# A transformer tower on one Trainium2 core: GpSimd adds two bias rows to whole tiles instead of TensorE passes with a selector row

## The chip, the cores and the metric

The kernel runs on one core of a Trainium2 chip. The metric is the time of one execution in microseconds, taken on the device. The engines are named TensorE (PE in the profile, PEld its weight loads), VectorE (DVE), ScalarE (ACT), GpSimd (POOL) and SyncE (SP, which here only starts DMAs).

## What is computed

A sequence of 129 rows (one class row, 128 rows made from the input by a state-space kernel) of 64 steps and 1024 columns goes through one layer: a layer norm, a narrow mixer (down to 128 columns, two rounds of a bidirectional state-space block, up to 1024), a residual, a second layer norm, and a feed-forward part of a base product plus routed low-rank experts. Cut to what touches the change:

```
def attn(x, ...):                    # x = layernorm(h)
    h = gelu(x @ w_down.T + b_down)
    ...                              # two state-space rounds, gate
    h = h @ w_up.T + b_up            # <- up bias
    return x + h

def ffn(x, ...):                     # x = layernorm(h)
    base_out = x @ base_W.T + base_b # <- base bias
    probs = softmax(x @ router_W.T + router_b)
    ...                              # top 8 of 15, low-rank experts
    return base_out + lora

h = tok(x, ...)
h = concat([cls_tok, h])
h = h + attn(layernorm(h), ...)
h = h + ffn(layernorm(h), ...)
```

## The kernel before

A tile is 128 partitions (two rows of the sequence, 64 steps each) by 1024 columns; there are 65 tiles, the last with the class row. The kernel is one software pipeline over iterations i = 0 to 69. In iteration i, tile i is made and normed (part A), tiles i-1 and i-2 are in the state-space rounds (H and G), tile i-4 gets its up product, residual and second norm (D), and tile i-5 its feed-forward part and its store (E). Iterations 8 to 61 stand in a loop of two, the others are written out. Every engine has its own hand-written order of steps, printed below at the end of each `body`, and waits on semaphores named after the steps (`wait(pool, i, tt=1)`: until tile i has its first `tt`).

The names that matter:

- `T` (two buffers): the new tile. GpSimd's `carry_h` (L908) makes `T * SD1 + NM1` of it, which is tile plus its first norm; the semaphore is `tt`. SP stores T to HBM (L801) and fetches it three iterations later as `T2` (L792). `carry_h` is the last step of GpSimd's iteration; ahead of it stand two decay products, `decays_back` (RB, L925), and additions of the narrow convolution, `add_bc`. Behind it the next iteration begins with `swap` (XSW, L846), `kernel_q` (V2, L853), `gram_back` (NB), `shift_imag`, `shift_none` and `skip` (XD, L885).
- `up` (TensorE, L1579): for each half of the columns four passes into one bank, the first of which is `mm(bT, row_sel, up_bias[:, c])`. `residual` (VectorE, L1401) adds the bank to `T2` and writes `HB`.
- `HB` (two buffers): what comes out of the first half. `norm_2` (ScalarE, L1016) norms it into T2, semaphore `xh2`. `turn_d` transposes that, and ScalarE and VectorE split it into `XHI` (`split_hi`) and `XLO` (`split_lo`, L1428).
- `bases` (TensorE, L1558): for each half of the columns 24 passes into bank `bO[h]`, and ahead of them `mm(bO[h], row_sel, base_bias[:, c])`. It waits for `xlo=2` of its tile.
- `final` (VectorE, L1448): adds `bO[h]` to HB, in place; SP then stores HB (L826). In VectorE's order, the end of an iteration is `split_lo(0)`, `final(0)`, `final(1)`, `split_lo(1)`; the next begins with `kernel_p` (VB, L1226), the gram products, `kernel_sum`, the mixing matrix Mt (L1287), and soon `add_skip` and `times_z` (XD).
- `mix` (TensorE, L1723) needs Mt. `turn_x` (L1647) transposes the input and needs XSW.

`row_sel` has ones in rows 0 and 32 and zeros elsewhere. Rows 0 and 32 of the 128-row tiles `up_bias` and `base_bias` hold the high and the low part of the bias, so that one TensorE pass lays the whole bias row on all 128 partitions of a bank. The prologue builds these: two loads to 64 rows, two ScalarE copies (L454, L455), two GpSimd subtractions (L345).

Of the kernel before, what the change touches and what calls it, by code (L numbers as in the profile page):

```python
# [38 lines left out]
def build(nc, x, cls_tok, log_dt, tok_B, inv_A_real, A_imag, w_down, b_down, w_up, b_up, gate1, in_w,  # L55
# [14 lines left out]
    BCP = 48  # L70
    BIAS_ROWS, BIAS_LO = 64, 32
    TILES = pairs + 1
    CLS = pairs

    with ExitStack() as keep:
# [23 lines left out]
        m_gt = sb("m_gt", [P, CS])  # L99
        row_sel = sb("row_sel", [P, P], F32R)  # L100
        up_bias = sb("up_bias", [P, HID], F32R)
        base_bias = sb("base_bias", [P, HID], F32R)
        rbias = sb("rbias", [P, NR])
# [31 lines left out]
        with ExitStack() as tmp:  # L135
# [18 lines left out]
            ones = ts("ones", [P, P])  # L154
            bias_s = ts("bias_s", [BIAS_ROWS, 2, HID])
            earlier0 = ts("earlier0", [P, P])
# [36 lines left out]
            s_zero, s_masks, s_consts = tsem("s_zero"), tsem("s_masks"), tsem("s_consts")  # L193
            s_bias, s_sel = tsem("s_bias"), tsem("s_sel")
            s_dup, s_par, s_tdt, s_exps = tsem("s_dup"), tsem("s_par"), tsem("s_tdt"), tsem("s_exps")
# [39 lines left out]
            def _(sp):  # L235
# [14 lines left out]
                for c in range(2):  # L250
                    small(cw[:, c, :], cwr[c * P:(c + 1) * P, :])
                    small(cb[:, c:c + 1], conv_b[c * P:(c + 1) * P].unsqueeze(1))
                small(bias_s[:, 0, :], b_up.unsqueeze(0).broadcast_to([BIAS_ROWS, HID]))
                small(bias_s[:, 1, :], base_b.unsqueeze(0).broadcast_to([BIAS_ROWS, HID]))
                small(rbias[:, :], router_b.unsqueeze(0).broadcast_to([P, NR]))
# [32 lines left out]
            def _(pool):  # L288
# [22 lines left out]
                for k, s in enumerate((512, 256, 768)):  # L311
                    pool.iota(lst_i[:, 32 + k:33 + k], pattern=[[1, 1]], base=s,
                              channel_multiplier=0).then_inc(s_consts, 1)
                pool.memset(row_sel[:, :].bitcast(F32), 0.0).then_inc(s_sel, 1)
                pool.memset(up_bias[:, :].bitcast(F32), 0.0).then_inc(s_sel, 1)
                pool.memset(base_bias[:, :].bitcast(F32), 0.0).then_inc(s_sel, 1)
                pool.wait_ge(s_sel, 3)
                for k, row in enumerate((0, BIAS_LO)):
                    pool.memset(row_sel[row:row + 1, :].bitcast(F32), 1.0).then_inc(s_sel, 1)
                    pool.wait_ge(s_sel, 4 + k)  # L320
                pool.memset(half_neg[:, :], -0.5)
# [19 lines left out]
                pool.wait_ge(s_onehot, NE)  # L341
                pool.wait_ge(s_bias, 2)
                for k, dst in enumerate((up_bias, base_bias)):
                    lo = slice(BIAS_LO, BIAS_ROWS)
                    link(TT(dst[lo, :], bias_s[lo, k, :], dst[lo, :].bitcast(F32), ALU.subtract))  # L345
                pool.wait_ge(s_albe, 1)
# [36 lines left out]
            def _(act):  # L383
# [58 lines left out]
                for c in range(CHUNKS):  # L442
                    if c % 2 == 0:
                        waves(c)
                        falls(c)
                    else:
                        falls(c)
                        waves(c)
                    if c == 0:
                        act.wait_ge(s_small, 16 * NSMALL)  # L450
                        act.wait_ge(s_sel, 3)
                        act.activation(alog[:, :], alog[:, :], ACT.Exp).then_inc(s_exps, 1)
                        act.activation(gt0[:, :], gate[:, :], ACT.Exp, scale=-1.0).then_inc(s_exps, 1)
                        act.activation(up_bias[0:BIAS_ROWS, :], bias_s[:, 0, :], ACT.Copy).then_inc(s_bias, 1)  # L454
                        act.activation(base_bias[0:BIAS_ROWS, :], bias_s[:, 1, :], ACT.Copy).then_inc(s_bias, 1)  # L455
                        while k < SMALL_JOBS:
                            nxt = evacuate(k, nxt)
                            k += 1
                    for _ in range(PER_CHUNK):
                        nxt = evacuate(k, nxt)  # L460
                        k += 1
# [5 lines left out]
            def _(dve):  # L467
# [156 lines left out]
                for c in range(CHUNKS):  # L624
# [82 lines left out]
        per = dict(cls_in=(1, 16), xswap=1, xt=1, xtc=1, wr=1, wi=2, wsum=1, v1=1, v2=1, vsum=1,  # L707
                   km=2, hev=4, st1=4, rs1=1, sd1=1, nm1=1, xh1=1, tt=1, tr1=2, xte=2, down=1, gelu=1,
                   pin=3, xms=1, conv0=4, conv=NCONV, cbm=TAPS - 1, cbc=TAPS - 1, dtc=NDT, asp=2, edt=1, xs=3, sz=1, trx=1, gram=1, xse=1,
# [60 lines left out]
        with nc.Block() as block:  # L770

            @block.sync
            def _(sp):
                def body(i, p):
                    if active(i, -1, CLS + 1) and not (isinstance(i, int) and not 1 < i + 1 < CLS):
                        load_x(i + 1, 1 - p)
                    if isinstance(i, int) and i == CLS:

                        wait(sp, i - 2, xh1=1)
                        wait_carry(sp, i - 2, p)  # L780
                        sp.dma_start(T[:, p, :], cls_tok[0].broadcast_to([P, HID])).then_inc(S["cls_in"].sem, 16)
                    if active(i, 5, TILES):
                        store(i - 5, 1 - p)
                    if active(i, 3, TILES):
                        src = at(carried, i - 3)

                        wait_carry(sp, i - 3, 1 - p)
                        wait(sp, i - 4, tr2=2)
                        apart(sp)
                        wait(sp, i - 4, gt=1)  # L790
                        apart(sp)
                        inc(sp.dma_start(T2[:, :], src[:, 0:HID]), "fetched")  # L792
                        inc(sp.dma_start(XM[:, :], src[:, HID:HID + P]), "fetched")
                    if active(i, 0, TILES):
                        dst = at(carried, i)
                        wait(sp, i, gelu=1)
                        apart(sp)
                        sp.dma_start(dst[:, HID:HID + P], U[:, p, 0, :]).then_inc(carry[p], 16)
                        wait(sp, i, tt=1)
                        apart(sp)  # L800
                        sp.dma_start(dst[:, 0:HID], T[:, p, :]).then_inc(carry[p], 16)  # L801
# [31 lines left out]
            def _(pool):  # L833
                def body(i, p):
# [65 lines left out]
                    def deviation_1():  # L900

                        if A1:
                            wait(pool, i, rs1=1)
                            wait(pool, i - 1, tt=1)
                            apart(pool)
                            inc(pool.tensor_scalar(SD1[:, :], RS1[:, :], 1.0, 1.0, ALU.mult, ALU.add), "sd1")

                    def carry_h():  # L908

                        if A1:  # L910
                            wait(pool, i, sd1=1, nm1=1, xh1=1)
                            apart(pool)
                            inc(pool.tensor_scalar(T[:, p, :], T[:, p, :], SD1[:, 0:1], NM1[:, 0:1], ALU.mult, ALU.add), "tt")

                    def root_2():
                        if D:
                            wait(pool, td, st2=4)
                            wait(pool, td - 1, xh2=1)
                            inc(pool.tensor_tensor(RS2[:, :], VE2[:, :], half_neg[:, 0:1], ALU.pow), "rs2")  # L919

                    def decays_back(part):
# [31 lines left out]
                    decays_back(1)  # L953
                    carry_h()


# [204 lines left out]
            def _(dve):  # L1161
                TT, TS, STT = dve.tensor_tensor, dve.tensor_scalar, dve.scalar_tensor_tensor

                def body(i, p):
# [209 lines left out]
                    def shift_1():  # L1374

                        if A1:
                            wait(dve, i, rs1=1)
                            wait(dve, i - 1, xh1=1, tt=1)
                            inc(STT(NM1[:, :], MV1[:, 0:1], -1.0, RS1[:, 0:1], ALU.mult, ALU.mult), "nm1")
# [68 lines left out]
                    def final(h):  # L1448
                        if E:
                            wait(dve, te, o=h + 1)  # L1450
                            c = slice(HALF * h, HALF * (h + 1))
# [79 lines left out]
            def _(pe):  # L1531
                mm, tr = pe.matmul, pe.transpose

                def body(i, p):
# [6 lines left out]
                    def ffn(c0, c1, bank, ks, last=None):  # L1541

                        for k in ks:
                            for n, (xs_, ws) in enumerate(((XHI, w_hi), (XHI, w_lo), (XLO, w_hi))):
                                ins = mm(bank[:, 0:c1 - c0], xs_[:, 1 - p, k, :], ws[:, k, c0:c1],  # L1545
                                         start=(c0 == HID and k == 0 and n == 0), stop=(last == k and n == 2))
                        return ins
# [10 lines left out]
                    def bases(h, a, b):  # L1558
                        if E:
                            if a == 0:  # L1560
                                wait(pe, te, xlo=2)
                                wait(pe, te - 1, fin=h + 1)
                                mm(bO[h][:, :], row_sel[:, :], base_bias[:, HALF * h:HALF * (h + 1)], start=True, stop=False)
                            ffn(HALF * h, HALF * (h + 1), bO[h], range(a, b))
# [14 lines left out]
                    def up(h):  # L1579
                        if D:  # L1580
# [5 lines left out]
                            c = slice(HALF * h, HALF * (h + 1))  # L1586
                            mm(bT[:, :], row_sel[:, :], up_bias[:, c], start=True, stop=False)
                            mm(bT[:, :], GTS[:, 0, :], wu_hi[:, c], start=False, stop=False)
                            mm(bT[:, :], GTS[:, 1, :], wu_hi[:, c], start=False, stop=False)
# [239 lines left out]
```

## Time and profile before

| what | before |
|---|---|
| median of 3 runs | 2318.59 us |
| lowest, highest | 2317.51, 2318.93 us |
| span of the profiled execution | 2315.8 us |
| TensorE busy | 2160.1 us, 93% |
| VectorE busy | 1843.7 us, 80% |
| ScalarE busy | 1527.5 us, 66% |
| GpSimd busy | 1095.6 us, 47% |

The profiled execution is a run of its own; only its span is known, the time from its first to its last instruction. Times in the timelines count from the start of the span. In a timeline row the columns are: start, duration, engine, line, operation, tiles written <- read, shape, count, and in brackets the idle time of the engine before it with what ended it. A TensorE pass is shown with its whole latency; the pitch, the distance between two starts, is what it costs in a row of passes. The granted clock is given as a share of 2.4 GHz; its two levels here are 1.0 and 0.5 (1.2 GHz).

### The profile page before, as it was taken

Reading aid. Unit: us, or ns where it says so; the run is one execution under the profiler, and the core shown is the slowest. Engines: PE = TensorE matmul, PEld = TensorE weight load, DVE = VectorE, ACT = ScalarE, POOL = GpSimd, SP = SyncE. Lnnn points to the kernel's source line nnn. Section 1 sums busy time; section 2 is a strip of 40 time slices with the busy share of each in tenths; the row PEclk is TensorE's granted clock in tenths of the full one; section 3 lists DMA queues with packets and bytes.
Section 4 is the critical chain, followed back from the end, with each engine's and each line's share of the span. In section 5 each row is a group of like instructions: output and inputs, shape, how many; then the busy total and the mean of one; then the engine's idle time right before and its main releaser. Section 6 shows DMA issues by size and latency. Waiting matters only on the chain.

```text
span 2315.8 us, 51899 instructions
## 1 busy us (share of the span) xinstructions
PE 2160.1 (93%) x14117; PEld 1805.7 (78%) x14117; DVE 1843.7 (80%) x4980; ACT 1527.5 (66%) x2921; POOL 1095.6 (47%) x1350
## 2 busy tenths in 40 slices
PE   2366999999999999999999999999999999999997
PEld 2245888888888888888888888888888888888776
DVE  8666788888888888888888888888888888887763
ACT  4465676667766677666777667676676766767552
POOL 5543554445544455444554445544455444554321
PEclk8577999999999999999999999999999999999999
DMA  5201111222112221122221222212222112221111
GB/s 150 65 26 36 56 51 47 64 64 64 50 46 64 64 64 58 37 64 64 64 61 35 64 64 64 63 34 61 64 64 64 35 60 64 64 64 38 62 40 34
DMA packets 90061, 132.61 MB, mean 57 GB/s; under 512 B 20379, under 2 KB 63559, under 8 KB 90006
## 3 DMA queue, kind: packets, MB, share of 16 engines
q1 hardware_dynamic: 87496, 126.12, 18.4%
q10 hardware_dynamic: 2510, 5.83, 0.8%
q8 instruction: 25, 0.41, 0.1%
q14 instruction: 30, 0.25, 0.0%
HBM read 55.17 MB, written 76.74 MB: 57 GB/s over the span
## 4 chain that ended last, share of the span: by engine, by line
issue 44%; PE 27%; POOL 9%; DVE 7%; ACT 6%; POOLq 1%; DVEq 0%; ACTq 0%
PE bank L1644 5%; PE bank L1545 5%; POOL CB L934 4%; PE bank L1600 3%; PE bank L1575 2%; DVE NF L1274 2%; ACT L1039 2%; POOL XD L885 2%; PE bank L1718 2%; PE bank L1702 2%; POOL RS L919 1%; PE bank L1577 1%; PE bank L1576 1%; POOL RS L898 1%; PE bank L1692 1%
## 5 line engine op out<-in xcount | busy, mean ns | idle before, releaser
L1545 PE MATMUL bank<-w_hi,XHI 128*128 128x512 f32 (+1 forms) x1560 | 623.0, 399 | 0.0
L1545 PE MATMUL bank<-w_lo,XHI 128*128 128x512 f32 (+1 forms) x1560 | 555.1, 356 | 0.0
L1545 PE MATMUL bank<-w_hi,XLO 128*128 128x512 f32 (+1 forms) x1560 | 554.6, 355 | 0.0
L1180 DVE SCALAR_TENSOR_TENSOR CX<-bank,cw,CX 128x252 f32<-128x252 f32 (+5 forms) x804 | 335.6, 459 | 62.2 <-ACT CX L977 62.0
L934 POOL TENSOR_TENSOR CB<-CB,CM 48x252 f32<-48x252 f32 (+5 forms) x402 | 293.1, 729 | 153.5 <-ACT CM L962 142.6
L1545 PEld LDWEIGHTS bank<-w_hi,XLO 128*128 128x128 f32 x1560 | 295.5, 189 | 46.9
L1545 PEld LDWEIGHTS bank<-w_lo,XHI 128*128 128x128 f32 x1560 | 297.0, 190 | 41.2
L1545 PEld LDWEIGHTS bank<-w_hi,XHI 128*128 128x128 f32 x1560 | 296.7, 190 | 41.2
L962 ACT ACTIVATE T<-bank 64x512 f32<-64x512 f32 x256 | 151.4, 591 | 261.9 <-PE bank L1634 257.2
L898 POOL TENSOR_TENSOR RS<-VE,half_neg 128x1 f32<-128x1 f32 x65 | 35.5, 546 | 370.7 <-DVE VE L1372 370.7
L925 POOL TENSOR_TENSOR RB<-m_gt,AS 128x512 fp32r<-128x512 f32 x134 | 165.0, 1231 | 56.9 <-DVE AS L1446 56.9
L962 ACT ACTIVATE CM<-CR,cwb 48x256 f32<-48x256 f32 x402 | 181.4, 497 | 3.7 <-POOL CB L934 1.5
L892 POOL TENSOR_TENSOR RS<-MS,half_neg 128x2 f32<-128x2 f32 x67 | 46.9, 700 | 244.2 <-DVE MS L1303 244.2
L1634 PE MATMUL bank<-VB,W 128*128 128x256 f32 x512 | 149.4, 416 | 7.8 <-DVE W L1245 5.8
L1428 DVE TENSOR_TENSOR XLO<-bank,XHI 128x512 fp32r<-128x512 f32 x130 | 89.9, 692 | 73.1 <-ACT XHI L962 73.1
L1434 DVE TENSOR_TENSOR RF<-m_lt,AS 128x512 fp32r<-128x512 f32 x134 | 142.8, 1104 | 0.0
L962 ACT ACTIVATE XHI<-bank 128x512 fp32r<-128x512 f32 x130 | 77.6, 597 | 95.3 <-PE bank L1600 95.3
L1644 PE MATMUL bank<-XHT,wdT 128*128 128x128 f32 x1040 | 135.4, 286 | 4.5 <-ACT XHT L962 4.5
L1644 PEld LDWEIGHTS bank<-XHT,wdT 128*128 128x128 f32 x1040 | 129.2, 202 | 6.1 <-ACT XHT L962 6.1
L877 POOL TENSOR_TENSOR NB<-GB,sp_dt 128x512 f32<-128x512 f32 x67 | 96.0, 1433 | 77.5 <-DVE GB L1257 77.5
L885 POOL TENSOR_TENSOR XD<-XS,DD 128x512 f32<-128x512 f32 x67 | 84.7, 1264 | 98.5 <-DVE DD L1265 53.2
L1292 DVE TENSOR_TENSOR XD<-bank,XD 128x512 f32<-128x512 f32 x67 | 46.4, 692 | 79.1 <-POOL XD L885 58.2
(295 smaller groups left out, 5375.1 us busy)
## 6 DMA issues: line engine op xcount, KB each, us to landing
carried<-T SPq DMA_DIRECT2D x65, 512.0 KB, 4.7
T<-carried SPq DMA_DIRECT2D x65, 512.0 KB, 3.8
out<-HB SPq DMA_DIRECT2D x129, 256.0 KB, 3.2
tables<-tab SPq DMA_DIRECT2D x8, 560.0 KB, 4.1
TB<-tables SPq DMA_DIRECT2D x64, 70.0 KB, 2.7
carried<-U SPq DMA_DIRECT2D x65, 64.0 KB, 3.5
XM<-carried SPq DMA_DIRECT2D x65, 64.0 KB, 4.7
XI<-in_x SPq DMA_DIRECT2D x128, 32.0 KB, 2.7
```

Of the source, the lines that this page charges most:

```text
L877: inc(pool.tensor_tensor(NB[:, :, :].rearrange("p (a h) t -> p a h t", a=2), GB[:, :, :].unsqueeze(2).broadcast_to([P, 2, NH, CS]), dtB, A ...
L885: inc(pool.tensor_tensor(XD[:, :, :], v3(XS[:, :], HD), DD[:, :].unsqueeze(2).broadcast_to([P, 2 * NH, HD]), ALU.mult), "xd")
L925: inc(pool.tensor_tensor(RB[:, part, :, :], m_gt[:, :].unsqueeze(1).broadcast_to([P, 2 * NH, CS]), decays(1, part), ALU.mult), "rb")
L934: inc(pool.tensor_tensor(CB[:, :, s:CS], CB[:, :, s:CS], CM[:, s % 3, :, 0:CS - s], ALU.add), "cbc")
L962: inc(act.activation(dst, src, ACT.Copy, scale=scale), name)
L1180: inc(STT(CX[:, c, :, s:CS], src[:, :, 0:CS - s], cw[:, c, k:k + 1], CX[:, c, :, s:CS], ALU.mult, ALU.add), "conv")
L1428: inc(TT(XLO[:, p, ks, :], v3(bT[:, :], P), XHI[:, p, ks, :].bitcast(F32), ALU.subtract), "xlo")
L1434: inc(TT(RF[:, part, :, :], m_lt[:, :].unsqueeze(1).broadcast_to([P, 2 * NH, CS]), decays(0, part), ALU.mult), "rf")
L1545: ins = mm(bank[:, 0:c1 - c0], xs_[:, 1 - p, k, :], ws[:, k, c0:c1], start=(c0 == HID and k == 0 and n == 0), stop=(last == k and n == 2))
L1600: ins = tr(bT[:, P * k:P * (k + 1)], T2[:, (4 * g + k) * P:(4 * g + k + 1) * P], ident[:, :])
L1634: ins = mm(bK[:, 256 * s:256 * (s + 1)], W[:, b, 2 * s:2 * s + 2, :].rearrange("p a c -> p (a c)"), VB[:, b, :, :].rearrange("p a c -> p ( ...
L1644: ins = mm(bK[:, 0:P], wdT[:, k, :], XHT[:, k, :], start=(k == 0), stop=(k == KC - 1))
```

## The change

The selector passes and all that builds them go. `up_bias` and `base_bias` become plain f32 tiles that hold the bias on all 128 partitions, loaded by DMA. GpSimd adds `up_bias` to T right behind the scaling in `carry_h` (so `tt` counts two), and `base_bias` to HB of tile i-5 in a new last step, `add_bias`, semaphore `hb`. All that waited for `tt=1` of a tile waits for `tt=2`: the carry store of SP, `deviation_1` of GpSimd and `shift_1` of VectorE for the tile after. `final` also waits for `hb`. In `bases` and `up` the first product pass now starts the accumulation.

```
-                small(bias_s[:, 0, :], b_up.unsqueeze(0).broadcast_to([BIAS_ROWS, HID]))
-                small(bias_s[:, 1, :], base_b.unsqueeze(0).broadcast_to([BIAS_ROWS, HID]))
+                small(up_bias[:, :], b_up.unsqueeze(0).broadcast_to([P, HID]))
+                small(base_bias[:, :], base_b.unsqueeze(0).broadcast_to([P, HID]))
...
-                        wait(sp, i, tt=1)
+                        wait(sp, i, tt=2)
...
                             inc(pool.tensor_scalar(T[:, p, :], T[:, p, :], SD1[:, 0:1], NM1[:, 0:1], ALU.mult, ALU.add), "tt")
+                            wait(pool, i, tt=1)
+                            inc(pool.tensor_tensor(T[:, p, :], T[:, p, :], up_bias[:, :], ALU.add), "tt")
...
+                    def add_bias():
+
+                        if active(i, 5, TILES):
+                            wait(pool, i - 5, xh2=1)
+                            inc(pool.tensor_tensor(HB[:, 1 - p, :], HB[:, 1 - p, :], base_bias[:, :], ALU.add), "hb")
...
                     decays_back(1)
                     carry_h()
+                    add_bias()
...
                         if E:
-                            wait(dve, te, o=h + 1)
+                            wait(dve, te, o=h + 1, hb=1)
                             c = slice(HALF * h, HALF * (h + 1))
                             inc(TT(HB[:, 1 - p, c], bO[h][:, :], HB[:, 1 - p, c], ALU.add), "fin")
...
-                                         start=(c0 == HID and k == 0 and n == 0), stop=(last == k and n == 2))
+                                         start=(k == 0 and n == 0), stop=(last == k and n == 2))
...
-                                mm(bO[h][:, :], row_sel[:, :], base_bias[:, HALF * h:HALF * (h + 1)], start=True, stop=False)
...
-                            mm(bT[:, :], row_sel[:, :], up_bias[:, c], start=True, stop=False)
-                            mm(bT[:, :], GTS[:, 0, :], wu_hi[:, c], start=False, stop=False)
+                            mm(bT[:, :], GTS[:, 0, :], wu_hi[:, c], start=True, stop=False)
```

## Rows read from the trace of the kernel before

**Rows 1.** The page's first part: busy time, share of the span, instructions.

```profile
PE 2160.1 (93%) x14117; PEld 1805.7 (78%) x14117; DVE 1843.7 (80%) x4980; ACT 1527.5 (66%) x2921; POOL 1095.6 (47%) x1350
```

**Rows 2.** Busy time by stretch: length, engines, granted clock, DMA share, GB/s.

```profile
1003.30:1067.50 64.20, 63.82 (x427) 53.70 (x427) 53.10 (x147) 44.81 (x87) 31.55 (x38) 1.00 0.19 57
```

**Rows 3.** Timeline of GpSimd at the seam of iterations 28 and 29.

```profile
1013.79 1.04 POOL L925 TENSOR_TENSOR RB<-m_gt,AS 128x512 fp32r<-128x512 f32 x1
1014.83 1.19 POOL L913 TENSOR_SCALAR T<-T,SD,NM 128x1024 f32<-128x1024 f32 x1
1015.97 0.29 POOL L846 COPY XSW<-XI 128x128 f32<-128x128 f32 x1
1016.22 1.06 POOL L853 TENSOR_TENSOR V<-TB 128x512 f32<-128x512 f32 x1
```

**Rows 4.** Timeline of VectorE, same seam.

```profile
1014.77 1.28 DVE L1452 TENSOR_TENSOR HB<-bank,HB 128x512 f32<-128x512 f32 x2
1016.29 0.69 DVE L1428 TENSOR_TENSOR XLO<-bank,XHI 128x512 fp32r<-128x512 f32 x1 [0.24 <-ACT XHI L962]
1016.90 0.93 DVE L1226 TENSOR_TENSOR VB<-TB 128x512 f32<-128x512 f32 x1
...
1018.15 0.68 DVE L1232 TENSOR_TENSOR VB<-VB,V 128x512 f32<-128x512 f32 x1
...
1021.55 0.69 DVE L1287 TENSOR_TENSOR Mt<-NF,EX 128x512 f32<-128x512 f32 x1
...
1025.11 0.69 DVE L1297 TENSOR_TENSOR XD<-XD,SZ 128x512 f32<-128x512 f32 x1
```

**Rows 5.** Timeline of TensorE, same seam, to `mix`.

```profile
1018.28 0.48 PE L1563 MATMUL bank<-base_bias,row_sel 128*128 128x512 f32 x1
1018.60 0.39 PE L1545 MATMUL bank<-w_hi,XHI 128*128 128x512 f32 x1
1018.83 0.40 PE L1545 MATMUL bank<-w_lo,XHI 128*128 128x512 f32 x1
...
1023.03 1.15 PE L1730 MATMUL bank<-XS,Mt 64*64 64x64 f32 x32
```

**Rows 6.** Timeline of ScalarE, same seam: evacuations of T, then squares.

```profile
1025.28 1.21 ACT L962 ACTIVATE T<-bank 64x512 f32<-64x512 f32 x2 [3.93 <-PE bank L1634]
1026.39 0.40 ACT L1060 ACTIVATE SQ<-XD 128x256 f32<-128x256 f32 x1
```

**Rows 7.** Timeline of GpSimd in the prologue: subtraction of two full operands.

```profile
30.80 2.36 POOL L345 TENSOR_TENSOR up_bias<-bias_s,up_bias 32x1024 fp32r<-32x1024 f32 x1
```

**Rows 8.** Busy time by stretch, columns as in rows 2: fill and tail.

```profile
181.60:188.40 6.80, 6.24 (x42) 5.21 (x43) 2.90 (x6) 2.09 (x6) 1.35 (x1) 0.50 0.01 2
...
215.70:219.10 3.40, 3.40 (x31) 2.87 (x27) 1.95 (x3) 0.14 (x1) 1.35 (x1) 0.51 0.00 0
...
2202.30:2205.70 3.40, 3.40 (x15) 3.01 (x13) 2.14 (x4) 2.47 (x3) 1.55 (x1) 0.50 0.92 241
```

**Rows 9.** Timeline of TensorE in the fill: `mix` behind an idle stretch.

```profile
182.16 1.98 PE L1730 MATMUL bank<-XS,Mt 64*64 64x64 f32 x32 [3.75 <-DVE Mt L1287]
...
215.29 1.62 PE L1730 MATMUL bank<-XS,Mt 64*64 64x64 f32 x32 [3.75 <-DVE Mt L1287]
```

**Rows 10.** Timeline of GpSimd: `carry_h` of iterations 5 and 64.

```profile
277.26 1.19 POOL L913 TENSOR_SCALAR T<-T,SD,NM 128x1024 f32<-128x1024 f32 x1
...
2168.77 1.21 POOL L913 TENSOR_SCALAR T<-T,SD,NM 128x1024 f32<-128x1024 f32 x1
```

**Rows 11.** Timeline of VectorE: `final` of iterations 5 and 64.

```profile
277.11 1.28 DVE L1452 TENSOR_TENSOR HB<-bank,HB 128x512 f32<-128x512 f32 x2
...
2168.62 1.28 DVE L1452 TENSOR_TENSOR HB<-bank,HB 128x512 f32<-128x512 f32 x2
```

**Rows 12.** Timeline of SyncE's queue at the seam of iterations 28 and 29.

```profile
1016.27 1.24 SPq L826 DMA_DIRECT2D out<-HB  x2
1018.07 0.36 SPq L792 DMA_DIRECT2D T<-carried  x1
```

More of the change, by code:

```diff
@@ L70, in build @@
     BCP = 48
-    BIAS_ROWS, BIAS_LO = 64, 32
     TILES = pairs + 1
@@ L99, in build @@
         m_gt = sb("m_gt", [P, CS])
-        row_sel = sb("row_sel", [P, P], F32R)
-        up_bias = sb("up_bias", [P, HID], F32R)
-        base_bias = sb("base_bias", [P, HID], F32R)
+        up_bias = sb("up_bias", [P, HID])
+        base_bias = sb("base_bias", [P, HID])
         rbias = sb("rbias", [P, NR])
@@ L154, in build @@
             ones = ts("ones", [P, P])
-            bias_s = ts("bias_s", [BIAS_ROWS, 2, HID])
             earlier0 = ts("earlier0", [P, P])
@@ L193, in build @@
             s_zero, s_masks, s_consts = tsem("s_zero"), tsem("s_masks"), tsem("s_consts")
-            s_bias, s_sel = tsem("s_bias"), tsem("s_sel")
             s_dup, s_par, s_tdt, s_exps = tsem("s_dup"), tsem("s_par"), tsem("s_tdt"), tsem("s_exps")
@@ L313, in _ @@
                               channel_multiplier=0).then_inc(s_consts, 1)
[L314 to L320, printed above, removed]
                 pool.memset(half_neg[:, :], -0.5)
@@ L341, in _ @@
                 pool.wait_ge(s_onehot, NE)
[L342 to L345, printed above, removed]
                 pool.wait_ge(s_albe, 1)
@@ L450, in _ @@
                         act.wait_ge(s_small, 16 * NSMALL)
-                        act.wait_ge(s_sel, 3)
                         act.activation(alog[:, :], alog[:, :], ACT.Exp).then_inc(s_exps, 1)
                         act.activation(gt0[:, :], gate[:, :], ACT.Exp, scale=-1.0).then_inc(s_exps, 1)
-                        act.activation(up_bias[0:BIAS_ROWS, :], bias_s[:, 0, :], ACT.Copy).then_inc(s_bias, 1)
-                        act.activation(base_bias[0:BIAS_ROWS, :], bias_s[:, 1, :], ACT.Copy).then_inc(s_bias, 1)
                         while k < SMALL_JOBS:
@@ L707, in build @@
         per = dict(cls_in=(1, 16), xswap=1, xt=1, xtc=1, wr=1, wi=2, wsum=1, v1=1, v2=1, vsum=1,
-                   km=2, hev=4, st1=4, rs1=1, sd1=1, nm1=1, xh1=1, tt=1, tr1=2, xte=2, down=1, gelu=1,
+                   km=2, hev=4, st1=4, rs1=1, sd1=1, nm1=1, xh1=1, tt=2, hb=1, tr1=2, xte=2, down=1, gelu=1,
                    pin=3, xms=1, conv0=4, conv=NCONV, cbm=TAPS - 1, cbc=TAPS - 1, dtc=NDT, asp=2, edt=1, xs=3, sz=1, trx=1, gram=1, xse=1,
@@ L903, in deviation_1 @@
                             wait(pool, i, rs1=1)
-                            wait(pool, i - 1, tt=1)
+                            wait(pool, i - 1, tt=2)
                             apart(pool)
@@ L1377, in shift_1 @@
                             wait(dve, i, rs1=1)
-                            wait(dve, i - 1, xh1=1, tt=1)
+                            wait(dve, i - 1, xh1=1, tt=2)
                             inc(STT(NM1[:, :], MV1[:, 0:1], -1.0, RS1[:, 0:1], ALU.mult, ALU.mult), "nm1")
```

## The prediction

> **What bounds the kernel now.** I read the page's busy shares first: TensorE 93%, VectorE 80%, GpSimd 47% [rows 1]. The reader should not stop there, since a share says nothing of who waits at a given spot. So next the busy time of two full iterations in the middle: TensorE works 63.82 of 64.20 us at full clock [rows 2]. The period is (2168.77 - 277.26)/59 = 32.06 us, from the carry operation of iterations 5 and 64 [rows 10]. TensorE fills it, so a pass that goes away could be worth its pitch. Last, the timelines of one iteration, engine beside engine, at the seam between two iterations, where both new operations are put [rows 3 to 5]. That is where the answer lies: at the seam GpSimd is not an idle engine. Its `carry_h` ends at 1016.02, while VectorE has started `final(0)` at 1014.77 [rows 3, 4]. The tile that the change wants added before `final` is thus queued behind work that already ends 1.25 us too late. In iterations 5 and 64 the same two operations stand 1.34 and 1.36 us apart [rows 10, 11]; these are the first and the last of 60 iterations that have both.
>
> **What is removed.** Four passes of 128x512 per iteration (two in `bases`, two in `up`). The pitch of such passes is 1018.83 - 1018.60 = 0.23 us [rows 5], so 0.93 us per iteration. Two of them lie between the seam and `mix`, which shortens that way of TensorE from 1023.03 - 1018.28 = 4.75 to 4.28 us [rows 5]. The two in `up` stand ahead of `residual`, where VectorE arrives from other work, and I count nothing for them. In the prologue two GpSimd subtractions (2 x 2.36 = 4.7 us, [rows 7]) and two ScalarE copies go, while two bias loads double to 512 KB each; I take 0 for the sum, within 4 us either way.
>
> **What is added, and its price.** Two GpSimd additions of 128x1024 f32 per tile, both operands full tiles. The nearest row is the prologue's subtraction of two full 1024-column operands: 2.36 us [rows 7], though on 32 partitions. The lower bound is twice a 128x512 operation with one repeated operand and a quiet VectorE, 2 x 1.04 = 2.08 us [rows 3]; the upper 2.6, the same row with another tenth for what a neighbour could take. I take 2.35, the row of the same form, and VectorE stands still during the additions.
>
> The Trainium skill (GPSIMD Engine Reference, section 3.1 and the table of 4.1) speaks against the change: ordinary two-input elementwise work belongs on VectorE. It gives 4497 ns for a 2048-column f32 addition; half of that is an estimate of 2.25 us, and by it the sum would be 0.2 us per iteration less.
>
> **Following the seam.** GpSimd: `carry_h` ends 1016.02; the second `tt` waits for the first's own signal, so it runs 1016.10 to 1018.45, and `hb` to 1020.80. `hb` itself needs only `xh2` of the iteration before, which is long there. VectorE: `final(0)` now waits for `hb` and starts at 1020.90 instead of 1014.77. Queued behind it are `final(1)`, the second `split_lo`, `kernel_p`, the gram products and the mixing matrix. The second `split_lo` had 0.24 us of waiting of its own [rows 4], which is swallowed: it starts at 1022.18, 5.89 late. `kernel_p` took 0.93 us with GpSimd's product running beside it [rows 3, 4]; that one will be over, which gives back 0.2. The mixing matrix, `skip` on GpSimd (it waits for VectorE) and `add_skip` thus come 5.7 us late. On GpSimd, `swap`, `kernel_q` and the rest are queued behind the additions too: XSW starts at 1020.80 instead of 1015.97, so TensorE's `turn_x`, just before 1018.28 [rows 5], waits until 1021.1.
>
> What of the 5.7 us stays? `times_z` ends at 1025.80 and ScalarE, busy with two evacuations, squares only at 1026.39 [rows 4, 6]: 0.5 of it is absorbed. From there (mean square, norm, transpose, output projection, `gt`, softplus, decays, back to `carry_h`) each step waits for the one before or VectorE works without a pause, so there is no cushion of size; it is a loop of dependences, and what enters it lengthens the period: 5.7 - 0.5 = 5.2 us.
>
> SP: `store` waits for `fin` and goes from 1016.27 to about 1022.3; the fetch of T2 behind it (1018.07, [rows 12]) becomes 1024, and `residual` uses T2 more than 10 us later. The carry store's `tt=2` is fulfilled at 1018.45, before SP comes to it. So the queue costs nothing. SD1 and NM1 of the next tile wait for `tt=2` as well, about 15 us after it.
>
> **TensorE's clock.** TensorE has next to nothing to do from 1018.3 to 1022.95, when the second `split_lo` is over: 4.6 us with two transposes in it. The kernel before shows what idle stretches do. Before `mix` at 182.16 and at 215.29 TensorE was idle 3.75 us [rows 9], and the granted clock was 0.50 for 6.8 us from 181.6, and 0.51 for 3.4 us from 215.7 [rows 8]: its lower level, 1.2 of 2.4 GHz. In the tail it was 0.50 for 3.4 us from 2202.3, after a thin stretch, and dense passes followed [rows 8]. The same `mix` then took 1.98 us instead of 1.15 [rows 5, 9]. I expect this in most iterations. At full clock TensorE comes to `mix` at 1022.95 + 4.28 = 1027.23, and the matrix, done at 1022.24 before [rows 4], is there at 1027.95, so 0.7 us of loss is covered. A low stretch of 3.4 us loses 1.7 us, one of 6.8 us 3.4; it may begin before the idle ends, as at 181.6, where 0.56 us of it fell into idle. I take 2.0, nearer to the short one since dense passes follow as at 2202.3. Then `mix` is at 1029.23, 6.2 us late, and the evacuations and squares behind it as much. By the two ends the shift is 5.9 and 7.6.
>
> The Trainium skill (TensorE: Matmul & The Clock Gate, Part 1, on HAM oscillation) says that a wait repeated in every tile can make the clock fall in every tile. The rows of the fill agree (3.75 us of idle, then 0.50); in the full iterations of before there is no such wait to see it in.
>
> **The sum.** 60 iterations x 6.2 = 372 us. Five fill iterations have only the first addition: `kernel_q` ends at 1019.6 instead of 1017.28 [rows 3], about 1.5 late for VectorE's `kernel_sum` at 1018.15 [rows 4], 0.9 after the cushion of ScalarE, 5 us in all. Four tail iterations have only `hb`, behind a decay product that ends at 1014.83 [rows 3]: 1014.83 + 2.45 - 1014.77 = 2.5, less 0.24 and 0.5, some 1.7 each, 7 us. Passes saved where TensorE bounds fill and tail: -4. Together 380 us. The profiled execution spans 2315.8 us, 2.8 below the median of the timed runs, 2318.6, which I take as lying around the span: 2315.8 + 380 + 2.8 = 2698.6, say **2698 us** (+16%).
>
> **Rivals.**
> - *The clock holds* (2639 us). The shift is 5.2: 60 x 5.2 + 8 = 320. For it: the two transposes break the idle stretch. Against: the idle of the fill was no longer, and the clock fell. With additions of 2.08 the shift is 4.66 and the time 2606.
> - *The low clock lasts* (2780 us). 6.8 us each time, 7.6 per iteration: 456 + 8. For it: the row at 181.6. Against: dense passes follow.
> - *The additions cost what a one-input operation costs* (2501 us). `carry_h` does 128x1024 in 1.19 us [rows 3]. Then both additions take 2.3 us less, the shift is 2.9 and TensorE's idle is short: 174 + 8. Against: the row of two full operands [rows 7].
> - *TensorE's passes decide* (2258 us, faster). If the additions ended before VectorE needs HB, the period would fall with TensorE: 65 x 0.93 = 60 us. It decides only if GpSimd is done by about 1014.77 + 0.24 + 0.5 = 1015.5, and without the additions it is done at 1016.0. What speaks for it is the full TensorE [rows 2] alone.
>
> **How the numbers follow.** Additions near 2.35 with a falling clock: 0.64 (2660 to 2765). The clock holds: 0.20. The low clock lasts: 0.07. One-input price: 0.05. Passes decide: 0.03. Nothing that shows: 0.01. The range is 2600 to 2765: it takes in the clock that holds with the cheap addition, and leaves out most of the low clock that lasts. What a measurement here tells from no change is about 0.2%: faster 0.03, within it 0.01, slower 0.96.
>
> **What would show it.** In the changed kernel: the two additions at 2.3 to 2.4 us, one behind the other; VectorE idle about 6 us before `final(0)`, ended by GpSimd's HB; TensorE idle before `turn_x` ended by XSW, and before `bases` ended by XLO; a period near 38.3 us; a granted clock that falls to 0.5 once per iteration, right behind the idle. If the clock stays at 1.00 the period is near 37.2. The prediction is wrong in its core if VectorE does not wait at `final(0)`, or if the period grows by less than 4 us although it waits.

## The result

The changed kernel takes 2690.98 us (median of 4 runs, 2687.54 to 2694.75) against 2318.76 us before: ratio 1.1607, 95% interval 1.159 to 1.1623. It is 16% slower. The profiled execution spans 2693.0 us, 377 more than before.

The page of the changed kernel, its busy shares and the slices of the granted clock (in tenths of full speed, 40 slices):

```profile
PE 2268.1 (84%) x13857; PEld 1851.5 (69%) x13857; DVE 1830.4 (68%) x4980; ACT 1529.1 (57%) x2919; POOL 1388.0 (52%) x1473
...
PEclk8567899899999999989999998999999999899888
```

TensorE has 260 passes fewer and yet is busy 108 us longer than in [rows 1]; GpSimd, with 5 us more work per iteration, still stands idle half of the time. Neither share shows why.

The seam is read from the timelines (start, duration, engine, line, operation). GpSimd:

```profile
1192.32 1.19 POOL L879 TENSOR_SCALAR T<-T,SD,NM 128x1024 f32<-128x1024 f32 x1
1193.59 2.37 POOL L881 TENSOR_TENSOR T<-T,up_bias 128x1024 f32<-128x1024 f32 x1
1195.91 2.34 POOL L893 TENSOR_TENSOR HB<-HB,base_bias 128x1024 f32<-128x1024 f32 x1
1198.20 0.29 POOL L812 COPY XSW<-XI 128x128 f32<-128x128 f32 x1
```

VectorE:

```profile
1198.36 1.29 DVE L1427 TENSOR_TENSOR HB<-bank,HB 128x512 f32<-128x512 f32 x2 [6.10 <-POOL HB L893]
1199.56 0.68 DVE L1403 TENSOR_TENSOR XLO<-bank,XHI 128x512 fp32r<-128x512 f32 x1
1200.16 0.68 DVE L1201 TENSOR_TENSOR VB<-TB 128x512 f32<-128x512 f32 x1
...
1204.56 0.69 DVE L1262 TENSOR_TENSOR Mt<-NF,EX 128x512 f32<-128x512 f32 x1
```

TensorE:

```profile
1198.54 0.47 PE L1625 MATMUL bank<-ident,XI 128*128 128x128 f32 x1 [2.61 <-POOL XSW L812]
...
1200.39 0.79 PE L1520 MATMUL bank<-w_hi,XHI 128*128 128x512 f32 x1 [1.16 <-DVE XLO L1403]
1200.98 0.63 PE L1520 MATMUL bank<-w_lo,XHI 128*128 128x512 f32 x1
...
1206.87 1.15 PE L1703 MATMUL bank<-XS,Mt 64*64 64x64 f32 x32
```

Measured from the start of `carry_h` in either kernel ([rows 3 to 6] and here), the steps stand as follows:

| step, from the start of `carry_h` | before | after | later by |
|---|---|---|---|
| XSW starts | 1.14 | 5.88 | 4.74 |
| `final(0)` starts | -0.06 | 6.04 | 6.10 |
| second `split_lo` starts | 1.46 | 7.24 | 5.78 |
| mixing matrix starts | 6.72 | 12.24 | 5.52 |
| `mix` starts | 8.20 | 14.55 | 6.35 |

Between the mixing matrix and `mix` the delay grows by 0.83 us. There the clock shows; busy time by stretch of the changed kernel, columns as in [rows 2]:

```profile
1198.20:1205.30 7.10, 5.60 (x16) 4.35 (x17) 6.87 (x11) 2.75 (x4) 4.67 (x6) 0.52 0.58 161
1205.30:1232.00 26.70, 26.29 (x174) 21.55 (x173) 19.43 (x63) 17.89 (x37) 11.08 (x15) 1.00 0.07 26
```

From 1198.20 to 1205.30 the granted clock is 0.52 (its lower level, 1.2 GHz), then full. Until 1198.54 TensorE had stood still for 2.61 us, and its next passes of any size begin at 1200.39; so some 2 us of the low stretch hold little work, and 5 us of it lie under `bases`. The period, from the `carry_h` of iterations 5 and 64 (rows below against [rows 10]), is (2526.77 - 277.00)/59 = 38.13 us instead of 32.06, 6.07 more.

```profile
277.00 1.19 POOL L879 TENSOR_SCALAR T<-T,SD,NM 128x1024 f32<-128x1024 f32 x1
...
2526.77 1.20 POOL L879 TENSOR_SCALAR T<-T,SD,NM 128x1024 f32<-128x1024 f32 x1
```

And the kernel's list of waits (who waited for whom, us in total, times, longest) has the two new ones near its top. The largest, ScalarE's for the bank that becomes T, stood in the kernel before too, with 257.2 us. 371.8 us in 62 times is the 6 us of each iteration.

```profile
ACT T L937 <- PE bank L1607: 438.3, 66, 8.2
DVE HB L1427 <- POOL HB L893: 371.8, 62, 6.4
...
PE bank L1625 <- POOL XSW L812: 154.6, 56, 7.0
```

### The profile page after: what moved, and what is told of

It is laid out like the page before. It is cut to its first block, busy times and chain, and to the rows that moved or that the text cites. A ratio compares the mean times of both kernels' runs of the same rounds, so it can differ in the third digit from the quotient of the medians.

```text
span 2693.0 us, 51709 instructions
## 1 busy us (share of the span) xinstructions
PE 2268.1 (84%) x13857; PEld 1851.5 (69%) x13857; DVE 1830.4 (68%) x4980; ACT 1529.1 (57%) x2919; POOL 1388.0 (52%) x1473
## 4 chain that ended last, share of the span: by engine, by line
issue 49%; POOL 24%; DVE 11%; PE 8%; ACT 2%; POOLq 1%; DVEq 1%; ACTq 0%
POOL CB L908 8%; POOL HB L893 5%; PE bank L1520 4%; DVE NF L1249 3%; POOL T L879 3%; POOL XD L851 3%; POOL RB L899 2%; DVE NF L1255 2%; DVE VB L1207 1%; DVE VB L1201 1%; POOL RS L864 1%; POOLq L36 1%; DVE XLO L1403 1%; PE bank L1607 1%; POOL W L835 1%
## 5 line engine op out<-in xcount | busy, mean ns | idle before, releaser
L1520 PE MATMUL bank<-w_hi,XHI 128*128 128x512 f32 (+1 forms) x1560 | 684.5, 439 | 93.0 <-DVE XLO L1403 93.0
L1520 PE MATMUL bank<-w_lo,XHI 128*128 128x512 f32 (+1 forms) x1560 | 605.1, 388 | 0.0
L1520 PE MATMUL bank<-w_hi,XLO 128*128 128x512 f32 (+1 forms) x1560 | 600.4, 385 | 0.0
L1520 PEld LDWEIGHTS bank<-w_hi,XHI 128*128 128x128 f32 x1560 | 337.8, 217 | 153.3 <-DVE HB L1427 90.6
L1520 PEld LDWEIGHTS bank<-w_hi,XLO 128*128 128x128 f32 x1560 | 330.2, 212 | 54.9
L1520 PEld LDWEIGHTS bank<-w_lo,XHI 128*128 128x128 f32 x1560 | 332.4, 213 | 42.1
L1427 DVE TENSOR_TENSOR HB<-bank,HB 128x512 f32<-128x512 f32 x130 | 83.8, 686 | 373.3 <-POOL HB L893 371.8
L881 POOL TENSOR_TENSOR T<-T,up_bias 128x1024 f32<-128x1024 f32 x65 | 154.7, 2380 | 5.4
L937 ACT ACTIVATE XTC<-bank 128x256 f32<-128x256 f32 x64 | 24.6, 384 | 233.9 <-PE bank L1626 233.9
L893 POOL TENSOR_TENSOR HB<-HB,base_bias 128x1024 f32<-128x1024 f32 x65 | 151.9, 2337 | 1.4 <-ACT T L991 1.4
```

The source lines that it names most:

```text
L881: inc(pool.tensor_tensor(T[:, p, :], T[:, p, :], up_bias[:, :], ALU.add), "tt")
L893: inc(pool.tensor_tensor(HB[:, 1 - p, :], HB[:, 1 - p, :], base_bias[:, :], ALU.add), "hb")
L937: inc(act.activation(dst, src, ACT.Copy, scale=scale), name)
L1427: inc(TT(HB[:, 1 - p, c], bO[h][:, :], HB[:, 1 - p, c], ALU.add), "fin")
```

## The experiments

The theory: the additions stand in a loop of dependences that runs through the seam, so what they delay there lengthens every iteration; the clock adds to it. The rivals: each addition costs its share wherever it stands; GpSimd's load or its traffic costs; TensorE's passes decide; the wait at `final` alone is the cost.

### The clock: TensorE kept busy in the idle stretch

The changed kernel with passes whose results are overwritten, ahead of and behind `turn_x`:

```
+                            wait(pe, i - 1, gelu=1)
+                            for _ in range(11):
+                                mm(bK[:, :], wu_hi[:, 0:P], wu_hi[:, 0:512], start=True, stop=True)
                             wait_x(pe, i, p)
                             wait(pe, i, xswap=1)
-                            wait(pe, i - 1, gelu=1)
...
+                            if E:
+                                wait(pe, te - 1, hwl=1)
+                                for _ in range(4):
+                                    mm(bR[:, :], wu_hi[:, 0:P], wu_hi[:, 0:512], start=True, stop=True)
```

> The changed kernel, with TensorE kept busy in its idle stretch: 11 passes of 128x512 into the bank of turn_x ahead of it, and 4 into the router's bank behind it, all overwritten later. Nothing else is moved, and no pass stands where TensorE had other work. If the low clock is what makes the period 38.13 instead of about 37.3, the clock stays at 1.00 and the period goes to 37.2 to 37.5: 2635 to 2655 us. If the clock costs nothing (the wait for the mixing matrix covers it), the time stays at 2691 within 0.3%.

Measured: 2664.3 us (2656.5 to 2665.0), ratio to before 1.1474 (1.1445 to 1.1502), 27 us less than the changed kernel. Busy time by stretch, first the changed kernel:

```profile
600.00:2000.00 1400.00, 1232.16 (x7664) 1008.24 (x7663) 965.77 (x2689) 826.60 (x1588) 750.89 (x773) 0.94 0.16 47
```

then the one with TensorE kept busy:

```profile
600.00:2000.00 1400.00, 1318.88 (x8385) 1069.29 (x8383) 983.66 (x2726) 834.97 (x1607) 761.61 (x782) 1.00 0.17 50
```

Its TensorE timeline at the seam:

```profile
1192.57 2.67 PE L1624 MATMUL bank<-wu_hi 128*128 128x512 f32 x11
1195.41 0.33 PE L1627 MATMUL bank<-ident,XI 128*128 128x128 f32 x1 [0.17 <-POOL XSW L812]
```

The granted clock stays at 1.00, and the kernel gets faster by doing more. So the low clock is a cost, and a small one. The `carry_h` of iterations 5 and 64:

```profile
290.22 1.19 POOL L879 TENSOR_SCALAR T<-T,SD,NM 128x1024 f32<-128x1024 f32 x1
...
2501.72 1.19 POOL L879 TENSOR_SCALAR T<-T,SD,NM 128x1024 f32<-128x1024 f32 x1
```

The period is (2501.72 - 290.22)/59 = 37.48 us, inside the expected 37.2 to 37.5, so the clock is 0.65 us of the 6.07 per iteration, and 5.42 remain. The time lies 9 us above its expected range all the same: the added passes lengthen the fill, and iteration 5 begins its `carry_h` at 290.22 instead of 277.00.

The same seam, VectorE, TensorE and ScalarE; its `carry_h` starts at 1189.13:

```profile
1201.43 0.69 DVE L1262 TENSOR_TENSOR Mt<-NF,EX 128x512 f32<-128x512 f32 x1
...
1202.27 1.15 PE L1709 MATMUL bank<-XS,Mt 64*64 64x64 f32 x32 [0.64 <-DVE Mt L1262]
...
1205.94 0.40 ACT L1035 ACTIVATE SQ<-XD 128x256 f32<-128x256 f32 x1
```

At full clock TensorE waits for the mixing matrix, 0.64 us. The matrix starts 12.30 us after `carry_h`, 5.58 later than before; ScalarE's squares start 16.81 us after it instead of 11.56 ([rows 6]), 5.25 later.

### One addition alone

With the up bias alone added by GpSimd (and the selector passes of the base bias kept), and with the base bias alone. The core of the two edits against the kernel before, first up alone:

```
-                            mm(bT[:, :], row_sel[:, :], up_bias[:, c], start=True, stop=False)
-                            mm(bT[:, :], GTS[:, 0, :], wu_hi[:, c], start=False, stop=False)
+                            mm(bT[:, :], GTS[:, 0, :], wu_hi[:, c], start=True, stop=False)
...
+                            wait(pool, i, tt=1)
+                            inc(pool.tensor_tensor(T[:, p, :], T[:, p, :], up_bias[:, :], ALU.add), "tt")
```

then base alone:

```
                     carry_h()
+                    add_bias()
...
-                            wait(dve, te, o=h + 1)
+                            wait(dve, te, o=h + 1, hb=1)
...
-                                mm(bO[h][:, :], row_sel[:, :], base_bias[:, HALF * h:HALF * (h + 1)], start=True, stop=False)
```

> Only the up bias is added by GpSimd (behind the scaling of T); the base bias stays a selector-row pass on TensorE. The theory (a loop of dependences through the seam): GpSimd's XSW and kernel_q come 2.4 us late, kernel_q ends at 1019.7 by the clock of the kernel before and holds up VectorE's kernel_sum by 1.5 us, ScalarE's cushion takes 0.5 of it, so the period grows by about 1.0 us: 2318.6 + 60 = 2379 us, range 2345 to 2400; no wait before final, granted clock 1.00. The rival that TensorE's passes decide: two passes fewer, 65 x 0.47 = 30 us less, 2288 us. The rival that each addition costs the same wherever it stands: half of the change's 372 us, 2505 us.

> Only the base bias is added by GpSimd, as its last step; the up bias stays a selector-row pass. The theory: hb ends at 1018.4 by the clock of the kernel before, final starts 3.7 us late; less 0.24 of split_lo's own wait, 0.2 of kernel_p and 0.5 of ScalarE's cushion, the period grows by 2.7 us at full clock: 2487 us. TensorE's idle is about 2 us and the clock falls in some iterations at most; with it up to 3.5 us and 2535. Expected 2495, range 2470 to 2540. Half of the change's cost would be 2505, so this run alone does not tell a sum of equal parts from the theory, but together with the up bias alone it does: the theory has 60 + 176, well short of 372.

Measured: up alone 2428.8 us (ratio 1.0474, 1.0448 to 1.0500), base alone 2509.2 us (1.0815, 1.0794 to 1.0835). Base alone is inside its range: 190 us against 176. Its `final(0)` starts 3.73 us after `carry_h` (1155.69), 3.79 late:

```profile
1159.42 1.29 DVE L1457 TENSOR_TENSOR HB<-bank,HB 128x512 f32<-128x512 f32 x2 [3.72 <-POOL HB L923]
```

Up alone cost 110 us instead of 60, outside its range. VectorE's timeline of up alone shows the steps that were missed:

```profile
1061.37 0.69 DVE L1428 TENSOR_TENSOR XLO<-bank,XHI 128x512 fp32r<-128x512 f32 x1 [0.24 <-ACT XHI L962]
1061.98 2.12 DVE L1226 TENSOR_TENSOR VB<-TB 128x512 f32<-128x512 f32 x1
...
1065.31 1.52 DVE L1232 TENSOR_TENSOR VB<-VB,V 128x512 f32<-128x512 f32 x1 [0.81 <-POOL V L851]
1066.75 1.32 DVE L1274 TENSOR_TENSOR NF<-GF,sp_dt 128x512 f32<-128x512 f32 x1
1068.10 0.69 DVE L1280 TENSOR_TENSOR NF<-NF,NB 128x512 f32<-128x512 f32 x1
1068.83 0.69 DVE L1287 TENSOR_TENSOR Mt<-NF,EX 128x512 f32<-128x512 f32 x1
```

beside GpSimd's:

```profile
1061.18 2.37 POOL L913 TENSOR_TENSOR T<-T,up_bias 128x1024 f32<-128x1024 f32 x1
1063.49 0.75 POOL L844 COPY XSW<-XI 128x128 f32<-128x128 f32 x1
1064.21 1.06 POOL L851 TENSOR_TENSOR V<-TB 128x512 f32<-128x512 f32 x1
1065.24 1.04 POOL L875 TENSOR_TENSOR NB<-GB,sp_dt 128x512 f32<-128x512 f32 x1
```

`kernel_p` takes 2.12 us, against 0.93 before and 0.68 in the changed kernel: it starts while GpSimd's addition runs and ends 0.55 us after it, about the length that it has alone. `kernel_sum` takes 1.52 instead of 0.68 beside GpSimd's next product NB, and it too ends 0.55 us after that. GpSimd's small copy takes 0.75 instead of 0.29 beside `kernel_p`. So some operations of VectorE and GpSimd, each working from SBUF to SBUF, hold each other up. In the changed kernel VectorE stands still at `final` during both additions, and `kernel_p` takes 0.68.

Not every longer row is a cost. `kernel_p` is in the shade of the wait for V that follows it (0.81 us). `kernel_sum` is 0.84 us longer, but the two products behind it (NF) take 1.32 and 0.69 us instead of 1.53 and 1.21 in the kernel before:

```profile
1018.75 1.53 DVE L1274 TENSOR_TENSOR NF<-GF,sp_dt 128x512 f32<-128x512 f32 x1
1020.31 1.21 DVE L1280 TENSOR_TENSOR NF<-NF,NB 128x512 f32<-128x512 f32 x1
```

There they stood beside GpSimd's NB and the product after it; here NB meets `kernel_sum` instead. What stays is the copy: XSW and with it V come some 0.5 us later than forecast, `kernel_sum` starts 2.08 us late (from the start of `carry_h`, 1059.91, against [rows 3, 4]) instead of 1.5, the mixing matrix 2.20, and the period, from the `carry_h` of iterations 5 and 64 (277.80 and 2281.06), grows by 1.90 us instead of 1.0. Of the 0.9 us more, 0.58 is this later start, some 0.1 what the longer and the shorter operations leave together, and the rest that less is absorbed behind them than the 0.5 us expected.

The two costs do not add up: 110 + 190 = 300 of 372 us. Alone, the up addition reaches VectorE only at `kernel_sum`, which before started 0.87 us after `kernel_q` had ended ([rows 3, 4]), so part of the delay is lost on the way; in the changed kernel it delays `final` in full, which starts 6.10 us late instead of 3.79 with base alone. And the low clock comes in most iterations only with the longer idle stretch: over 600:2000 us the mean clock is 1.00, 0.98 and 0.94 in up alone, base alone and both.

### The wait at `final`, taken from what is queued behind the additions

The second addition, of the same size, now writes to a tile that nobody reads; `final` does not wait for it, and the base bias is left out. Against the changed kernel:

```
-                            inc(pool.tensor_tensor(HB[:, 1 - p, :], HB[:, 1 - p, :], base_bias[:, :], ALU.add), "hb")
+                            wait(pool, i - 6, hb=1)
+                            inc(pool.tensor_tensor(SCR[:, :], up_bias[:, :], base_bias[:, :], ALU.add), "hb")
...
-                            wait(dve, te, o=h + 1, hb=1)
+                            wait(dve, te, o=h + 1)
```

> The changed kernel, whose last GpSimd step writes its sum (same size, two full operands) to a tile that nobody reads, and final does not wait for it; the base bias is left out of the result. It tells the wait at final from what is queued behind the additions on GpSimd. If the wait at final is the cost, only what the up addition alone costs is left: about 2430 us. If the queue costs as much (XSW and kernel_q 4.8 us late, VectorE's kernel_p and kernel_sum held up by them), the mixing matrix still comes some 4.8 us late, the period grows by about 4.3 us and the time is 2570 to 2620 us.

Measured: 2570.7 us, ratio 1.1103 (1.1083 to 1.1122). The period, from the `carry_h` of iterations 5 and 64 (275.86 and 2419.95), is 36.34 us, 4.28 more than before: as the queue was expected to cost. VectorE does not wait at `final` any more, and waits one step further on:

```profile
1149.33 1.28 DVE L1429 TENSOR_TENSOR HB<-bank,HB 128x512 f32<-128x512 f32 x2
1150.94 0.69 DVE L1405 TENSOR_TENSOR XLO<-bank,XHI 128x512 fp32r<-128x512 f32 x1 [0.34 <-ACT XHI L939]
1151.60 2.06 DVE L1203 TENSOR_TENSOR VB<-TB 128x512 f32<-128x512 f32 x1
...
1157.15 1.52 DVE L1209 TENSOR_TENSOR VB<-VB,V 128x512 f32<-128x512 f32 x1 [3.10 <-POOL V L820]
```

GpSimd's two additions beside it:

```profile
1150.73 2.38 POOL L882 TENSOR_TENSOR T<-T,up_bias 128x1024 f32<-128x1024 f32 x1
1153.07 2.79 POOL L895 TENSOR_TENSOR SCR<-up_bias,base_bias 128x1024 f32<-128x1024 f32 x1
```

So the biggest new wait in the list is not the cost of the change: without it, 252 of the 372 us are still there, because `kernel_q` and XSW are queued behind the additions on the same engine. A little of that is new in this run: the second addition takes 2.79 us instead of 2.34, since `kernel_p` gets in between the two. (`kernel_p`, 2.06 us here, lies in the shade of the 3.10 us for which VectorE then waits for V; the longer `kernel_sum` is largely made up for by the NF products, 1.32 and 0.69 us as in up alone.) The reverse, the wait at `final` without the queue, was not run.

### The addition moved off the seam

The changed kernel with `add_bias` behind `root_y`, where GpSimd waits 5.6 us in every iteration:

```
                     root_y()
+                    add_bias()
                     root_1()
...
                     carry_h()
-                    add_bias()
```

> The changed kernel with the base-bias addition moved in GpSimd's order from the end to behind root_y, where GpSimd is idle for 5.6 us; same work, same passes removed. The theory (the place at the seam costs, not the addition): only the up addition is left at the seam, so as with the up bias alone, about 2370 us, range 2340 to 2395, no wait before final. The rival that GpSimd's added work or its traffic beside VectorE costs: above 2450 us.

Measured: 2427.9 us, ratio 1.0474 (1.0450 to 1.0498). The same addition, 2.40 us long in its new place, now costs no more than the two TensorE passes that it replaces: the time is that of up alone (2428.8), which keeps them. The place costs, not the addition. That both lie above the expected range has the same cause: here too the copy takes 0.75 us (median) behind the held-up `kernel_p`.

### Both additions off the seam, and what the passes are worth

Both behind `root_y`, the up bias for the tile of the iteration before; SP stores T an iteration later:

```
+                    def add_up():
+                        if active(i, 1, TILES):
+                            wait(pool, i - 1, tt=1)
+                            inc(pool.tensor_tensor(T[:, 1 - p, :], T[:, 1 - p, :], up_bias[:, :], ALU.add), "tt")
...
                     root_y()
+                    add_bias()
+                    add_up()
                     root_1()
...
+                    if active(i, 1, TILES):
+                        wait(sp, i - 1, tt=2)
+                        apart(sp)
+                        sp.dma_start(at(carried, i - 1)[:, 0:HID], T[:, 1 - p, :]).then_inc(carry[1 - p], 16)
                     if active(i, 5, TILES):
                         store(i - 5, 1 - p)
```

Beside it a kernel with the passes removed and no addition at all:

```
-                            wait(pool, i, tt=1)
-                            inc(pool.tensor_tensor(T[:, p, :], T[:, p, :], up_bias[:, :], ALU.add), "tt")
...
                     carry_h()
-                    add_bias()
```

> Both additions moved behind root_y into GpSimd's idle time: base bias of tile i-5, then up bias of tile i-1; SP stores T one iteration later, ahead of the store of HB. The seam is then as in the kernel before, with four TensorE passes fewer per iteration. If TensorE sets the period, 65 x 0.93 = 60 us less: 2258 us. If the loop of dependences sets it as much as TensorE, only the part of the passes on that loop is saved: 2285 to 2318 us; I expect 2295. Slower than 2325 would mean that additions beside VectorE's convolution cost something.

> The changed kernel without the two additions: both biases are left out of the result. It measures what the four removed passes are worth by themselves. TensorE sets the period: 2258 us. The loop of dependences sets it as much: 2285 to 2318 us. The prediction counted about nothing for the passes inside the loop. If the additions behind root_y are hidden entirely, this time is the same as theirs within 0.2%.

Measured: without additions 2297.9 us, ratio 0.9902 (0.9883 to 0.9922); both off the seam 2381.8 us, ratio 1.0265 (1.0246 to 1.0284). The first says what 260 passes are worth here: 20 us of the 60 that their pitch adds up to. TensorE is busy for 1375.34 of the 1400 us from 600 to 2000 and still does not set the period by itself. The second was a miss: 84 us above the kernel without additions, though nothing is added at the seam. Among VectorE's operations one has another length than in the kernel without additions, `gated_a`, which scales a 128x128 tile from SBUF to SBUF (min, median and max in ns, first and last start):

```profile
L1365 DVE TENSOR_SCALAR XM<-XM,al x65: 271/1790/1901, 221.0 to 2337.6; 128x128 f32<-128x128 f32 x65
```

GpSimd's timeline in that kernel:

```profile
1083.35 2.39 POOL L891 TENSOR_TENSOR T<-T,up_bias 128x1024 f32<-128x1024 f32 x1
```

and VectorE's beside it:

```profile
1083.44 0.68 DVE L1344 BATCH_NORM_STATS2 ST<-T 128x6 f32<-128x512 f32 x1
1084.04 1.79 DVE L1365 TENSOR_SCALAR XM<-XM,al 128x128 f32<-128x128 f32 x1
```

It ends just after the second addition does (1085.74), at 1085.83. The statistics of T ahead of it (0.68 us) are as long as ever. So `gated_a` was moved out of the additions' way, in VectorE's order:

```
                     mean_square()
+                    gated_a()
                     conv(1, 0)
...
                     stats_1(0)
-                    gated_a()
```

> The kernel with both additions behind root_y took 2381.8 us, though nothing is added at the seam; in its trace VectorE's gated_a (XM, 128x128, SBUF to SBUF) takes 1.79 us instead of 0.27 and ends with GpSimd's second addition. Here gated_a is moved in VectorE's order to behind mean_square, ahead of the additions; nothing else changes. If VectorE is held up by GpSimd's operation there, and that is the whole cost, the time is that of the kernel without additions: 2298 us, range 2288 to 2312, faster than the kernel before by 0.9%. If the cost is GpSimd's added load, or the later store of T, it stays near 2380.

Measured: 2303.3 us, ratio 0.9945 (0.9928 to 0.9962): 0.6% faster than the kernel before, and 5 us above the kernel without additions, where both off the seam stood 84 us above it. The line of `gated_a` in it, against 1790 ns in the median above:

```profile
L1365 DVE TENSOR_SCALAR XM<-XM,al x65: 279/286/288, 217.3 to 2257.7; 128x128 f32<-128x128 f32 x65
```

Beside the up addition in it (GpSimd's row first), the operation LG, which reads a bank:

```profile
1019.28 2.38 POOL L891 TENSOR_TENSOR T<-T,up_bias 128x1024 f32<-128x1024 f32 x1
...
1019.95 0.15 DVE L1310 TENSOR_TENSOR LG<-bank,rbias 128x15 f32<-128x15 f32 x1
```

So some 5 us of GpSimd's work per iteration cost about 5 us in the whole kernel, where nothing waits for it and it holds up no operation of VectorE. The single runs of the two kernels overlap (2298.9 to 2311.6 and 2293.1 to 2302.5), so even the 5 us are not certain.

## Why the prediction was right

The predicted 2698 us stand 7 us above the measured 2691. The mechanism is the one forecast; that the sum is so close is in part luck, since its terms are off in both directions. Point by point:

- **The price of the additions** was right: 2.37 and 2.34 us, against 2.35 taken from [rows 7]. That row, 32 partitions wide, held for 128. The bound from the 512-column product with a repeated operand (2.08) would have been low. The estimate of 2.25 us from the Trainium skill (GPSIMD Engine Reference, section 3.1) is 4 to 5% low; the trace decides.
- **The seam** was right step by step: `final(0)` 6.10 late (6.13 forecast), the second `split_lo` 5.78 (5.89), the mixing matrix 5.52 (5.7), XSW 5.88 after the start of `carry_h` (5.97).
- **The loop** was right in kind: what enters at the seam comes back as period. Without the low clock the shift is 5.42 us (measured with TensorE kept busy), 5.2 forecast. There the mixing matrix comes 5.58 late and the squares 5.25, so 0.33 of the 0.5 us that the evacuations were to absorb shows at that seam. TensorE waits 0.64 us for the matrix, where 0.7 was forecast.
- **The clock** was right in kind and too dear: it falls at the idle stretch, as forecast from [rows 8, 9], and costs 0.65 us per iteration instead of 1.0. The mean clock of 0.94 from 600 to 2000 is by an estimate 4 to 5 us at the lower level per iteration (0.06 x 2 x 38.13), and the 2.0 us of loss taken stood for 4; in the seam shown, some 2 us of the low stretch fall where TensorE has little to do, against 0.56 us in the fill. This and the point above go opposite ways, which is why the sum, 6.07 against 6.2, is closer than its terms.
- **Fill and tail** were taken as 8 us. By the spans of the profiled executions they are 377 - 60 x 6.07 = 13. The fill shows none of it (`carry_h` of iteration 5 at 277.00, before 277.26); it lies in the tail, which has five iterations with `hb` alone (65 to 69) and not four.
- **What is removed**: nothing was counted for the passes beyond the shorter way to `mix` and 4 us in fill and tail; by themselves they are worth 20 us in the kernel before. The rival that they decide (2258 us) falls: even without the additions the time is 2298.
- **Which path carries it**: the prediction followed the wait at `final` and mentioned `swap` and `kernel_q` as also late. The run without that wait shows that the second path by itself would cost 4.28 of the 6.07 us (0.45 of GpSimd's time in it being the longer second addition, which the changed kernel does not have). For the time it made no difference; as an account of the cause it was one-sided.
- **What was not seen**: that GpSimd's addition and VectorE's operations hold each other up. The sign stood in [rows 3, 4]: `kernel_q` ends at 1017.28 and `kernel_p` at 1017.83, 0.55 us after it, the same distance as in up alone; the prediction read it as a slowdown of 0.2 us. The changed kernel was spared, because VectorE stands still meanwhile; the expectations for the up bias alone and for both off the seam were not, by 50 and 87 us.

That the loop of dependences closes as described is shown by the runs at the seam and off it: what is late at the squares comes back as period (5.25 and 5.42 us with TensorE kept busy). The steps between the squares and the next `carry_h` were not taken apart.

## What to carry to other kernels

An engine with half of its time free is not free at a given place: look which of its operations the next step waits for, and put new work where it idles and where nobody waits, not at the end of its order. When VectorE and GpSimd both work from SBUF to SBUF, look also at which operations of the other engine would run beside the new one; moving one 0.27 us operation out of its way was worth 78 us here. And take the largest new wait of a list as a place to look, not as a price: without it two thirds of the cost stayed.

## What the runs showed of the hardware

Some of VectorE's operations from SBUF to SBUF end only behind a GpSimd operation that runs beside them: `kernel_p` took 2.12 us instead of 0.68 with GpSimd's 2.37 us addition beside it and ended 0.55 us after it, `gated_a` 1.79 instead of 0.27, ending 0.09 us after. GpSimd is held up in turn: its copy took 0.75 instead of 0.29 us, an addition 2.79 instead of 2.34. Operations that read a bank were not held up beside the same additions (`split_lo` 0.69 in up alone, LG 0.15 in the last kernel), nor were the statistics of T (0.68).

The Trainium skill (SBUF — State Buffer, "SBUF: two separate sides") describes a port pair that VectorE and GpSimd lock for a whole instruction, the loser waiting; on VectorE's side it names operations with two SBUF inputs or in a two-port mode. The rows agree for `kernel_p` and `kernel_sum`, whose two inputs lie in SBUF, and for GpSimd's copy; that `gated_a`, with one input tile, ran in such a mode is not shown by any run.
